# The rows of a second layer norm made by ScalarE instead of GpSimd, inside an attention and expert kernel

## The reference, cut to what matters

```
x = x + cross_attention(layernorm(x), ctx)       # 2048 tokens, width 256, 16 heads of 16, 77 keys
x = x + ffn(layernorm(x))

layernorm(x) = (x - mean(x)) / sqrt(var(x) + 1e-5)

ffn(x): scores = sigmoid(x @ gate_w.T)           # 8 experts
        sel    = top_k(scores + expert_bias, 2)
        shared = silu(x @ sw1.T) * (x @ sw3.T) @ sw2.T
        routed = for each token and chosen expert the same form with that expert's weights,
                 its input and its output times the score
        return shared + routed
```

## Time and profile before

| | |
|---|---|
| median of 3 runs | 317.82 us (317.42 to 320.69) |
| the profiled execution | 320.79 us, of which the span from first to last instruction is 319.1 us |
| PE busy | 277.7 us (87% of the span), PEld 242.6 us |
| DVE busy | 197.5 us (62%) |
| ACT busy | 154.7 us (48%) |
| POOL busy | 150.9 us (47%) |
| mean granted TensorE clock | 0.96 of full speed |

### The profile page before, as it was taken

How to read it: one execution, slowest core, us unless ns; L and a number is a source line. 1 busy time by engine, 2 the same in 40 slices (tenths; PEclk the granted TensorE clock), 3 DMA queues, 4 the chain that set the end, 5 groups by cost and what they waited for, 6 DMA issues and landing times.

```text
span 319.1 us, 6451 instructions
## 1 busy us (share of the span) xinstructions
PE 277.7 (87%) x1961; PEld 242.6 (76%) x1961; DVE 197.5 (62%) x683; ACT 154.7 (48%) x384; POOL 150.9 (47%) x223
## 2 busy tenths in 40 slices
PE   4879999999999999989868899999999999997100
PEld 4567888888888888868657688888888888886000
DVE  1557555577756776755755877666666666664085
ACT  2145666666666666573322344556566555655000
POOL 8000666666689989986671400333333443333200
PEclk9999999999999999999995999999999999999855
DMA  7069622222213333111021432233333333321399
GB/s 220 3 97 386 217 66 68 67 67 67 66 46 112 102 94 102 67 37 67 35 102 36 152 97 73 84 102 102 118 102 103 112 104 103 101 81 54 103 378 342
DMA packets 27324, 35.37 MB, mean 111 GB/s; under 512 B 8123, under 2 KB 18619, under 8 KB 27291
## 3 DMA queue, kind: packets, MB, share of 16 engines
q1 hardware_dynamic: 18496, 22.59, 23.9%
q0 software_dynamic: 3408, 9.41, 8.4%
q10 hardware_dynamic: 5387, 2.95, 3.1%
HBM read 22.07 MB, written 12.87 MB: 110 GB/s over the span
## 4 chain that ended last, share of the span: by engine, by line
PE 62%; POOL 14%; DVE 9%; DMA 5%; issue 4%; ACT 3%; SPq 1%; POOLq 0%
PE psum L849 13%; PE psum L851 12%; PE psum L850 12%; PE psum L855 7%; PE psum L918 5%; POOL w_lo L361 5%; POOL lists L351 4%; DMA w_hi<-results 3%; POOL rows L342 3%; PE psum L873 3%; PE psum L907 2%; PE psum L934 2%; DVE row_max L681 2%; ACT probs L412 1%; POOL rstd L338 1%
## 5 line engine op out<-in xcount | busy, mean ns | idle before, releaser
L384 POOL DMA_INDIRECT results<-probs_t,place x39 | 37.4, 959 | 80.4 <-ACT probs_t L468 80.4
L849 PE MATMUL psum<-w_lo,x_hi 128*128 (+1 forms) x110 | 48.5, 441 | 0.7 <-DVE x_lo L715 0.7
L850 PE MATMUL psum<-w_hi,x_lo 128*128 (+1 forms) x110 | 44.0, 400 | 0.0
L851 PE MATMUL psum<-w_hi,x_hi 128*128 (+1 forms) x110 | 43.9, 399 | 0.0
L918 PEld LDWEIGHTS psum<-vals,probs_t 128*128 128x128 f32 x320 | 38.8, 194 | 2.9 <-issue 2.5
L918 PE MATMUL psum<-vals,probs_t 128*128 128x51 f32 x320 | 40.3, 274 | 0.0
L849 PE MATMUL psum<-w_lo,h_hi 128*128 (+1 forms) x110 | 32.4, 295 | 8.6 <-DVE h_lo L731 4.5
L351 POOL DMA_INDIRECT lists<-rows,dest x32 | 32.1, 1002 | 15.8 <-issue 8.2
L361 POOL TENSOR_TENSOR w_lo<-w_stage,w_hi 128x256 fp32r<-128x256 f32 x54 | 38.0, 735 | 0.1
L731 DVE TENSOR_TENSOR h_lo<-psum,h_hi 128x256 fp32r<-128x256 f32 x55 | 23.3, 423 | 22.5 <-ACT h_hi L398 21.8
L456 ACT ACTIVATE act_s<-psum,share 128x256 f32<-128x256 f32 x39 | 18.5, 474 | 32.2 <-issue 25.2
(11 more groups left out here) (147 smaller groups left out, 627.5 us busy)
## 6 DMA issues: line engine op xcount, KB each, us to landing
w_stage<-in_ffn SPq DMA_DIRECT2D x27, 256.0 KB, 2.7
probs<-lists SPq DMA_DIRECT2D x39, 131.0 KB
w_hi<-results SPq DMA_DIRECT2D x7, 512.0 KB, 6.4
out_x<-resid ACTq DMA_DIRECT2D x7, 256.0 KB, 6.4
lists<-pad_rows SPq DMA_DIRECT2D x9, 131.0 KB
x_t<-in_xt SPq DMA_DIRECT2D x1, 896.0 KB, 10.5
resid<-in_x SPq DMA_DIRECT2D x1, 896.0 KB, 12.3
x_t<-in_xt SPq DMA_DIRECT2D x1, 768.0 KB, 4.7
```

The lines of the kernel that those rows point to most:

```text
L384: pool.indirect_dma_start(results, bass.IndirectOffsetOnAxis(ap=place[:, j:j + 1], axis=0), y_rows[:, cols(par)], None).then_inc(b_out[par ...
L849: mm(to, ah, bl, start=start, stop=False, skip_group_check=not group)
L850: mm(to, al, bh, start=False, stop=False, skip_group_check=not group)
L851: return mm(to, ah, bh, start=False, stop=stop and group, skip_group_check=not group)
```

## The change

The rows are made by ScalarE, as `Identity(rstd * x + shift)` with `shift = -mean * rstd`, where GpSimd made them as `(x - mean) * rstd`. GpSimd keeps the power and multiplies a `[128, 1]` column, VectorE makes `-mean`. ScalarE's instruction is placed between the two exponentials. On TensorE the transposition of the rows moves from ahead of the first four transpositions of the probabilities to behind the transposition of the attention. For tiles 14 and 15, in the second stage, ScalarE's instruction stands behind `silu(0)` and behind `step_b(1)`.

```diff
+            def norm_scale(t):                                        # POOL
+                pool.wait_ge(s["ln2_step"], 4 * (t + 1))
                 pool.tensor_tensor(rstd2[:, t:t + 1], ve2[:, t:t + 1], minus_half[:, :],
                                    ALU.pow).then_inc(s["rstd2_done"], 1)
-                pool.wait_ge(s["rstd2_done"], t + 1)
-                need(pool, scat[slot], 16 * TOPK * (t // ROW_BUFS))
-                pool.tensor_scalar(rows[:, slot * ROW:slot * ROW + DIM], resid[:, cols(t)],
-                                   mv2[:, 2 * t:2 * t + 1], rstd2[:, t:t + 1],
-                                   ALU.subtract, ALU.mult).then_inc(s["xn2_done"], 1)
+                pool.wait_ge(s["rstd2_done"], 2 * t + 1)
+                pool.tensor_tensor(shift2[:, t:t + 1], minus_mean[:, :], rstd2[:, t:t + 1],
+                                   ALU.mult).then_inc(s["rstd2_done"], 1)
...
+            def normed_rows(t):                                       # ACT
+                slot = t % ROW_BUFS
+                act.wait_ge(s["rstd2_done"], 2 * t + 2)
+                need(act, scat[slot], 16 * TOPK * (t // ROW_BUFS))
+                act.activation(rows[:, slot * ROW:slot * ROW + DIM], resid[:, cols(t)], ACT.Identity,
+                               scale=rstd2[:, t:t + 1], bias=shift2[:, t:t + 1]).then_inc(s["xn2_done"], 1)
...
                 exponentials(i, 0)
+                if live(i - 2):
+                    normed_rows(i - 2)
                 exponentials(i, 1)
...
             def residual_mean(t):                                     # DVE
-                dve.wait_ge(s["ln2_step"], 3 * t + 1)
+                need(dve, s["rstd2_done"], 2 * t)
+                dve.wait_ge(s["ln2_step"], 4 * t + 1)
...
+                ts(minus_mean[:, :], mv2[:, 2 * t:2 * t + 1], -1.0, None, ALU.mult).then_inc(s["ln2_step"], 1)
...
                 if live(i + 1):                                       # PE
                     queries(i + 1)
-                if live(i - 2):
-                    normed_transposed(i - 2)
                 pe.wait_ge(s["exped"], 2 * i + 1)
                 probs_transposed(i, 0, 4)
                 if live(i - 1):
                     attn_transposed(i - 1)
+                if live(i - 2):
+                    normed_transposed(i - 2)
                 pe.wait_ge(s["exped"], 2 * i + 2)
                 probs_transposed(i, 4, CHUNKS)
```

More of the change, by code:

```diff
@@ L163, in layer_kernel @@
     stats2, mv2, rstd2 = sb("stats2", 6), sb("mv2", 2 * TILES), sb("rstd2", TILES)
+    shift2, minus_mean = sb("shift2", TILES), sb("minus_mean", 1)
     q_hi, q_lo = sb("q_hi", DIM, F32R), sb("q_lo", DIM, F32R)
@@ L333, in query_scale @@
                                    ALU.pow).then_inc(s["rstd1_done"], 1)
-            def normed_rows(t):
-                slot = t % ROW_BUFS
-                pool.wait_ge(s["ln2_step"], 3 * (t + 1))
+            def norm_scale(t):
+                pool.wait_ge(s["ln2_step"], 4 * (t + 1))
                 pool.tensor_tensor(rstd2[:, t:t + 1], ve2[:, t:t + 1], minus_half[:, :],
                                    ALU.pow).then_inc(s["rstd2_done"], 1)
-                pool.wait_ge(s["rstd2_done"], t + 1)
-                need(pool, scat[slot], 16 * TOPK * (t // ROW_BUFS))
-                pool.tensor_scalar(rows[:, slot * ROW:slot * ROW + DIM], resid[:, cols(t)],
-                                   mv2[:, 2 * t:2 * t + 1], rstd2[:, t:t + 1],
-                                   ALU.subtract, ALU.mult).then_inc(s["xn2_done"], 1)
+                pool.wait_ge(s["rstd2_done"], 2 * t + 1)
+                pool.tensor_tensor(shift2[:, t:t + 1], minus_mean[:, :], rstd2[:, t:t + 1],
+                                   ALU.mult).then_inc(s["rstd2_done"], 1)
             def scatter(t):
@@ L366, in _ @@
                 if live(i - 2):
-                    normed_rows(i - 2)
+                    norm_scale(i - 2)
                 if i >= SCATTER_LAG:
@@ L374, in _ @@
             scatter(TILES - SCATTER_LAG)
-            normed_rows(TILES - 2)
+            norm_scale(TILES - 2)
             scatter(TILES - SCATTER_LAG + 1)
-            normed_rows(TILES - 1)
+            norm_scale(TILES - 1)
             for t in range(TILES - SCATTER_LAG + 2, TILES):
@@ L496, in _ @@
             silu(0)
+            normed_rows(TILES - 2)
             x_high(2)
@@ L503, in _ @@
             step_b(1)
+            normed_rows(TILES - 1)
             step_b(2)
@@ L560, in residual_mean @@
             def residual_mean(t):
-                dve.wait_ge(s["ln2_step"], 3 * t + 1)
+                need(dve, s["rstd2_done"], 2 * t)
+                dve.wait_ge(s["ln2_step"], 4 * t + 1)
                 dve.bn_aggr(mv2[:, 2 * t:2 * t + 2], stats2[:, :]).then_inc(s["ln2_step"], 1)
             def residual_variance(t):
-                dve.wait_ge(s["ln2_step"], 3 * t + 2)
+                dve.wait_ge(s["ln2_step"], 4 * t + 2)
                 ts(ve2[:, t:t + 1], mv2[:, 2 * t + 1:2 * t + 2], EPS, None, ALU.add).then_inc(s["ln2_step"], 1)
+                ts(minus_mean[:, :], mv2[:, 2 * t:2 * t + 1], -1.0, None, ALU.mult).then_inc(s["ln2_step"], 1)
             def divided(t):
```

## The result

The changed kernel takes 326.61 us (median of 4 runs, 326.08 to 327.57), the kernel before 318.15 us (4 runs): +8.46 us, ratio 1.0259, 95% interval 1.0215 to 1.0302. Slower, as forecast, but the prediction was 323.4 us and its range ended at 326.2. The profiled execution took 327.09 us, its span is 325.3 us. Medians here are over all runs of a kernel, but ratios and intervals leave out the slow ones, those over 1.5% above the fastest run of the same kernel.

What follows compares the result with a forecast made beforehand. The prediction took the loop of PE and ACT, 7.90 us per iteration, as the bound. +6.4 us for the pace, −0.25 for DVE's router work and −0.5 at the attention stage's end gave +5.6, 323.4 us; range 320.3 to 326.2.

Steps and rivals of the forecast that it cites:

- What bounds the kernel: Attention loop: PE and ACT need 7.90 us per iteration; freeing POOL gives under 1 us in all.
- ScalarE's instruction: Between the two exponentials: takes 507 to 598 ns, 598 taken; ACT's string grows by 0.49 us.
- The moved transposition: On PE, behind the attention's: `x_t` can start 0.50 us later by this alone, not adding to ACT's delay.
- The pace: Attention loop: projection loads 0.46 us later, an iteration takes 8.36 us; over fourteen iterations +6.4 us.
- POOL and the waits on it: In the loop: column multiplication takes 0.20 us, ACT never waits for the shift, POOL's lighter work costs nothing.
- DVE's router work: Iteration 6 to 7: router work no longer meets POOL's weights, −0.25 us; nothing more from iteration 9 on.
- The end of the attention stage: First `x_lo` pair at 140.96 us: POOL will be past its subtractions by then, −0.5 us.
- The sum: Whole kernel: +6.4 − 0.25 − 0.5 = +5.6 us, giving 323.4 us on the median.
- C: Rival, 88 to 138 us: POOL was the limit; seven iterations give 4 us, 313.8 us; chance 0.05.
- E: Rival, ahead of the second exponential: ACT waits for the shift, +0.3 us × 14 on top, 327.6 us; chance 0.05.
- B: Rival, attention loop: half the delay is real, transposition ready sooner and instruction cheaper; +2.8 us, 320.6 us; chance 0.14.
- D: Rival: stall at 164 us goes, 4 us plus some 2 us for the clock, 317.4 us; chance 0.06.

Runs made afterwards that it cites:

- pe_late: Kernel before with only TensorE's new order (rows' transposition behind the attention's), rows still by GpSimd: 327.7 us, ratio 1.0114.
- act_extra: Kernel before plus an extra ScalarE instruction of the new kind between the exponentials, result unused: 334.42 us, ratio 1.0292.
- after_parts: Changed kernel with expert-weight splitting dealt out differently, none in iterations 11 and 14: 323.27 us, ratio 1.0117 to the kernel before.
- before_parts: Kernel before with expert-weight splitting dealt out differently, none in iterations 11 and 14: 319.62 us, ratio 1.0016.
- after_pause_parts: Changed kernel, TensorE's old order, ScalarE's rows in its pause before the peaks, no weights in iterations 11 and 14: 328.55 us, ratio 1.0080.
- after_early: Changed kernel with TensorE's old order, rows still by ScalarE: 326.18 us, ratio 1.0242 to the kernel before.
- after_copy_early: Changed kernel with TensorE's old order and a plain copy as ScalarE's instruction: 322.06 us, ratio 1.009 to the kernel before.
- after_pause: Changed kernel with TensorE's old order and ScalarE's rows in its pause ahead of the peaks' copy: 332.3 us, ratio 1.0203.

## Why the prediction was wrong, step by step

*What bounds the kernel.* Right. The loop of PE and ACT set 7.90 us, and taking all weights from POOL in iterations 11 and 14 did not lower it (7.89 and 7.88 us).

*ScalarE's instruction.* Right. Forecast 598 ns, measured 591 (L439), and 0.50 us from its start to that of the second exponential. The Trainium skill, "ScalarE: Activation LUTs", section "What ACT_TABLE_LOAD costs", leads to an estimated 585 ns; the trace agrees.

*The moved transposition.* The mechanism was right, the size too high: 0.32 us alone instead of 0.46. It did not matter, since the two causes don't add.

*The pace.* Forecast 8.36, measured 8.35 us.

*POOL and the waits on it.* Right: L341 took 190 ns (forecast 200), and in the loop ScalarE never waits for the shift.

*DVE's router work, the step that failed.* "From iteration 9 on POOL's scatter still lies across the router's work, so I leave it at 0.25": I let these iterations keep their old excess. The 0.25 us was gained in iterations 6 and 7 (their excess of 0.28 us is gone). (It would have gone with any longer pace: steps 6 to 7 of `pe_late` and `act_extra` have no excess either, though `score` takes 0.59 and 0.79 us there.) But the router's work starts 0.5 us later by the same delay of `q_hi` that I had worked out, and in 11 and 14 more of DVE's operations than before meet POOL's work. The number stood in my text; I did not lay the intervals of the two engines over each other for iteration 11, and the range had no term for a loss there. `act_extra` shows that this delay alone brings the loss, with POOL's work where it was. In the changed kernel POOL's subtractions start 1.1 us sooner; the wait behind iteration 11 is shorter there than in `act_extra` (0.76 us against 1.21), and the one behind 14 longer (0.78 against 0.53). Steps 11 to 12, 12 to 13 and 14 to 15 cost 0.50 + 1.46 + 0.51 = 2.47 us beyond the pace, of which 1.16 us is the clock. `after_parts` shows that the meeting with POOL's subtractions is what costs: with these out of the way in 11 and 14, the three steps are 0.79, 1.16 and 0.81 us shorter.

*The end of the attention stage.* The pair `x_lo` takes 0.76 instead of 1.47 us, as forecast, so that gain was there:

```profile
152.76 0.76 DVE L726 TENSOR_TENSOR x_lo<-x_t,x_hi 128x256 fp32r<-128x256 f32 x2 [3.06 <-ACT x_hi L450]
```

But PE was at the lower clock there after its wait in iteration 15, and the gain can't be seen in the sum.

*The sum.* From iteration 2 to 15 the first profiles differ by 8.05 us: 13 × 0.45 = 5.85, −0.28, +2.47. With iteration 15's own 0.45 that is 8.5 us, against 8.46 us in the timed runs. That the two agree is luck. The spans of the same two profiles differ by 6.2 us: +2.1 us ahead of iteration 2, where step 1 to 2 took 10.01 us instead of 8.31 at half clock, +8.05, and −4.0 us behind iteration 15. It is by luck too that the time lies only 0.41 us above the range, since the missing term is 2.47 us. What stays open is the rest of the program. From the peaks of iteration 15 to the end the kernel before took 183.0 and 184.5 us in two profiles, the changed one 179.0, 187.6 and 187.3. It varies by more than any effect of the change that I could name there, in the same kernel, with the stall near 164 us and the stretches of half clock. I did not find what causes the stall.

*The rivals.* C (POOL as the limit) is out by `before_parts`, E (waits on POOL) by the rows, B by the pace (that a pair is ready sooner than its modelled end, the first half of B, is what `pe_late` shows). D happened in the first profile of the changed kernel, where PE has no wait over 1.6 us between 160 and 192 us, against 3.8 before, but not in the second and third.

## What to carry to other kernels

An engine that fills the chain of waits may only be level with another loop; look for a stretch where it idles and compare the pace before taking work from it. Where an engine's string has 0.09 us of slack, an instruction of 0.59 us cost 0.45 us (its length, less 0.10 of overlap and 0.04 of slack), and did not lengthen the string in the pause two instructions earlier. When one engine's work moves against another's, lay their new intervals over each other in every iteration that has extra work, not only in the plain one: a delay of 0.5 us brought a wait of 1.21 us here.

## What the hardware did that I had not expected

Small DVE operations on 128x64 or 128x32 elements take 0.2 us alone and 0.65 to 0.72 us while POOL subtracts weights. POOL's scatter does it too: a cast of 8 columns goes from 0.17 to 0.68 us beside it in `act_extra`. A copy of 8 columns goes from 0.16 to 0.64 us beside the subtractions. Waits of 0.76 to 0.78 us on TensorE were followed by the lower clock in three profiles of the changed kernel, and so was one of 0.62 us in `after_pause_parts`. Waits of 0.78 us in iteration 12 of `after_early` (one of 0.79 in its iteration 15 was), 0.98 in `after_copy_early` and 1.21 in `act_extra` were not, so the length of the wait does not decide it; what does stays open. A fall cost 1.16 us in step 12 to 13, and 1.6 us in a plain step (9.72 instead of 8.12 in `after_pause`, 9.46 instead of 7.90 in the second profile of the kernel before).
